# Attention's output from packed rows, its biases folded into one row, and the first transfers issued inside the first normalization

## What is computed

```
x = x + xattn(layernorm(x), ctx)          # W_Q b_Q W_K b_K W_V b_V W_O b_O
   Q = (x W_Q + b_Q), K = (ctx W_K + b_K), V = (ctx W_V + b_V), by head
   out = concat_h( softmax(Q K^T / 4) V ) W_O + b_O
x = x + ssm(layernorm(x), ...)
x = x + experts(layernorm(x), ...)
```

## Time and profile before

| | |
|---|---|
| median of 3 runs | 2363.89 us |
| the profiled execution's own time | 2363.51 us |
| its span, first to last instruction | 2361.8 us |
| TensorE busy | 2154.9 us (91%) |
| VectorE / ScalarE / GpSimd busy | 61% / 52% / 34% |
| mean granted TensorE clock | 0.956 of full |

### The profile page before, as it was taken

The page is one execution under the profiler, slowest core; times in us unless marked ns, Lnnn a source line. Parts: engine busy times, 40 slices in busy tenths (PEclk is TensorE's granted clock), DMA queues, the critical chain, the costliest instruction groups (busy, mean ns, idle before and its releaser), DMA issues. The chain is left out here.

```text
span 2361.8 us, 65032 instructions
## 1 busy us (share of the span) xinstructions
PE 2154.9 (91%) x28672; PEld 1768.7 (75%) x28672; DVE 1444.9 (61%) x2610; ACT 1239.7 (52%) x1667; POOL 797.4 (34%) x571
## 2 busy tenths in 40 slices
PE   5999999999999999999999997896799997499993
PEld 3789999999999999999999995643233336499993
DVE  4655556555555555565555552427588875688885
ACT  2355555555555555555555553363799971255661
POOL 2222222222222222222222212012699962255551
PEclk8999999999999999999999998987899998699997
DMA  2111111111111111111111103004875521466663
GB/s 90 36 49 46 40 48 39 47 42 39 47 42 40 51 42 41 48 39 47 41 39 48 43 16 103 4 5 185 216 173 145 143 81 55 158 223 224 223 221 123
DMA packets 130685, 197.40 MB, mean 84 GB/s; under 512 B 17714, under 2 KB 108850, under 8 KB 130243
## 3 DMA queue, kind: packets, MB, share of 16 engines
q1 hardware_dynamic: 120594, 176.58, 24.9%
q0 software_dynamic: 4416, 12.06, 1.5%
q10 hardware_dynamic: 5392, 4.59, 0.6%
HBM read 161.60 MB, written 31.59 MB: 82 GB/s over the span
## 5 line engine op out<-in xcount | busy, mean ns | idle before, releaser
L507 DVE TENSOR_REDUCE max_part<-work 128x1 f32<-128x384 f32 (+1 forms) x1024 | 539.2, 570 | 239.7 <-PE work L635 216.2
L570 ACT ACTIVATE probs<-scores 128x1024 f32<-128x1024 f32 (+1 forms) x416 | 423.8, 1026 | 397.5 <-PE scores L660 381.5
L467 POOL TENSOR_TENSOR ctx_lo<-ctx_whole,ctx_hi 128x768 fp32r<-128x768 f32 (+1 forms) x128 | 232.3, 1815 | 1034.2 <-DVE ctx_hi L490 1034.2
L502 DVE SCALAR_TENSOR_TENSOR keys_lo<-work,bk,keys_hi 128x384 fp32r<-128x384 f32 (+1 forms) x256 | 162.6, 636 | 262.2 <-ACT keys_hi L549 262.2
L1193 POOL TENSOR_TENSOR decay<-steps_in,xn 128x1024 f32<-128x1024 f32 x126 | 243.2, 1965 | 53.4 <-DMA steps_in<-scratch_results 39.7
L625 PE MATMUL work<-wv_hi,ctx_hi 128*128 128x256 f32 (+1 forms) x832 | 243.9, 293 | 2.1
L654 PE MATMUL scores<-q_hi,keys_hi 64*128 64x256 f32 (+1 forms) x1664 | 241.9, 283 | 0.0
L654 PE MATMUL scores<-q_lo,keys_hi 64*128 64x256 f32 (+1 forms) x1664 | 237.2, 277 | 0.0
L654 PE MATMUL scores<-q_hi,keys_lo 64*128 64x256 f32 (+1 forms) x1664 | 237.1, 277 | 0.0
L625 PE MATMUL work<-wv_hi,ctx_lo 128*128 128x256 f32 (+1 forms) x832 | 234.4, 282 | 0.0
L674 PE MATMUL acc<-probs,values 128*17 128x64 f32 x13312 | 230.5, 220 | 4.0 <-ACT probs L570 4.0
(11 more groups left out here) (234 smaller groups left out, 4685.4 us busy)
## 6 DMA issues: line engine op xcount, KB each, us to landing
xs<-in_w_T SPq DMA_DIRECT2D x46, 1024.0 KB
ctx_whole<-in_ctx_T SPq DMA_DIRECT2D x96, 384.0 KB, 3.2
steps_in<-scratch_results SPq DMA_DIRECT2D x256, 128.0 KB, 2.7
ctx_whole<-in_ctx_T SPq DMA_DIRECT2D x32, 449.0 KB, 3.5
scratch_results<-steps SPq DMA_DIRECT2D x16, 512.0 KB, 2.6
scratch_mixed<-mixed ACTq DMA_DIRECT2D x32, 128.0 KB, 1.7
mixed_b<-scratch_mixed SPq DMA_DIRECT2D x4, 1024.0 KB, 13.6
scratch_z<-z SPq DMA_DIRECT2D x16, 256.0 KB, 2.5
```

What stands on the lines that cost most here:

```text
L467: nc.gpsimd.tensor_tensor(ctx_lo[c][:, :, 0:n], s.ctx_whole[c % 2][:, :, 0:n], ctx_hi[c][:, :, 0:n].bitcast(F32), ALU.subtract).then_inc(l ...
L502: nc.vector.scalar_tensor_tensor(keys_lo[par][:, m, start:start + n], bank[:, 0:n], s.bk[:, m:m + 1], keys_hi[par][:, m, start:start + n]. ...
L507: nc.vector.reduce_max(max_part[par][:, place(pair), c:c + 1], bank[:, 0:CHUNKS[c][1]], AX) \
L570: nc.scalar.activation(probs[slot][0:rows, :], scores[slot][0:rows, :], ACT.Exp, scale=1.0 / HD ** 0.5).then_inc(exp_done, 1)
```

## The change

1. `load_constants` is gone. Its transfers become `sp_start` of the first normalization and its identity part of `pool_start`. W_O, b_V and b_O are loaded there as well, ahead of the context.
2. b_V W_O is made once at the end of that block: VectorE widens b_V to 128 equal columns, TensorE multiplies it by W_O (two matmuls of 256 columns), VectorE adds it to `bo`, which holds b_O in every partition.
3. In attention, GpSimd adds `bo` to four tiles of `x_tok` at the end of each of the passes b = 2 to 5.
4. The head groups' places in the columns of the result are permuted (`mixed_column`), and `attention_output` loads only filled rows, packed: 8 transfers of 16 partitions x 8 batches x 128 columns for each group (32 in place of 4). `mixed_b`, `mixed_T` and `wo` are half as large. `row_of` is made by VectorE from `ident` in four pieces. A token tile is spread by 4 matmuls of 128 columns, the two halves into output partitions 0 to 63 and 64 to 127, and projected by 2 matmuls, each tile as soon as it is divided.
5. ScalarE's bias and loads, GpSimd's clearing, selector and addition leave the block.

```diff
-TOKENS_LOADED, MIXED_LOADED, RESULTS_LOADED = 16, 32, 48
+TOKENS_LOADED, MIXED_LOADED, RESULTS_LOADED = 16, 16 * 9, 16 * 10
...
+            sp.dma_start(s.wo[:, :, :], d.W_O.rearrange("(a p) n -> p a n", p=P)).then_inc(s.o_loaded, 16)
+            sp.dma_start(s.bv[:, :], column_tiles(d.b_V), allow_slow_non_contiguous=True).then_inc(s.o_loaded, 16)
+            sp.dma_start(s.bo[:, :], d.b_O.rearrange("(a n) -> a n", a=1).to_broadcast([P, DIM])).then_inc(s.o_loaded, 16)
+            sp.wait_ge(context_padded, 1)
             for c in range(2):
                 load_context(sp, d, s, 0, c)
...
+            dve.wait_ge(s.o_loaded, 48)
+            nc.vector.tensor_copy(bv_wide[:, :, :], s.bv[:, :].rearrange("p (g a) -> p g a", a=1)
+                                  .to_broadcast([P, KD, P])).then_inc(bv_widened, 1)
+            dve.wait_ge(bias_projected, 1)
+            nc.vector.tensor_tensor(s.bo[:, :], s.bo[:, :], banks[0][:, 0:DIM], ALU.add)
+
+        def project_bias(pe):
+            pe.wait_ge(s.o_loaded, 48)
+            pe.wait_ge(bv_widened, 1)
+            pe.wait_ge(copied, KD * LN_GROUPS - 3)
+            for g in range(KD):
+                last = nc.tensor.matmul(banks[0][:, 0:DIM], bv_wide[:, g, :], s.wo[:, g, :],
+                                        start=(g == 0), stop=(g == KD - 1))
+            last.then_inc(bias_projected, 1)
...
+            def add_bias(first, last):
+                for t in range(first, last):
+                    nc.gpsimd.tensor_tensor(s.x_tok[:, t, :], s.x_tok[:, t, :], s.bo[:, :], ALU.add)
+
             prepare(0, 0)
             for b in range(1, batches):
                 prepare(b, b % 2, more=b + 1 < batches)
+                if 2 <= b < 2 + LN_GROUPS:
+                    add_bias((b - 2) * GT, (b - 1) * GT)
...
-                sp.dma_start(mixed[:, batches, :, :].rearrange("p b g l -> p b (g l)"),
-                             d.mixed.rearrange("b p n -> p b n")[:, batches, :]).then_inc(s.group_loaded[c], 16)
+                for half in range(2):
+                    for j in range(HPG):
+                        first = half * SIDE + j * HD
+                        sp.dma_start(mixed[first:first + HD, batches, :],
+                                     d.mixed.rearrange("b p n -> p b n")[32 * j:32 * j + HD, batches,
+                                                                         half * P:(half + 1) * P]) \
+                            .then_inc(s.group_loaded[c], 16)
...
-        def add_values_bias(act, c):
-            act.wait_ge(divided, CT * (c + 1))
-            for g in range(G):
-                part = mixed_T[:, g, c * BANK:(c + 1) * BANK]
-                nc.scalar.activation(part, part, ACT.Identity, bias=bv[:, g:g + 1]).then_inc(biased, 1)
...
-            nc.gpsimd.memset(row_of[:, :, :], 0.0).then_inc(row_of_made, 1)
-            pool.wait_ge(row_of_made, 1)
-            nc.gpsimd.affine_select(out=row_of[:, :, :], in_=row_of[:, :, :], compare_op=ALU.not_equal, fill=1.0,
-                                    base=0, pattern=[[-1, P], [0, 32]], channel_multiplier=1) \
-                .then_inc(row_of_made, 1)
-            pool.wait_ge(loaded, 16 * 9)
-            nc.gpsimd.tensor_tensor(s.x_tok[:, :, :], s.x_tok[:, :, :],
-                                    bo[:, :].rearrange("p (a n) -> p a n", a=1).to_broadcast([P, TT, DIM]), ALU.add) \
-                .then_inc(bias_added, 1)
...
-                    last = nc.tensor.matmul(spread[t % SPREAD_RING][:, i, :],
-                                            row_of[:, 4 * b:4 * b + 4, :].rearrange("p j i -> p (j i)"), inverse[:, :],
-                                            start=True, stop=True)
+                    for half in range(2):
+                        last = nc.tensor.matmul(spread[t % SPREAD_RING][half * SIDE:(half + 1) * SIDE, i, :],
+                                                row_of[:, 4 * b:4 * b + 4, :].rearrange("p j i -> p (j i)"),
+                                                inverse[:, half * P:(half + 1) * P],
+                                                start=True, stop=True, skip_group_check=True)
...
-            pe.wait_ge(biased, G * (c + 1))
             for t in range(CT * c, CT * (c + 1)):
+                pe.wait_ge(divided, t + 1)
...
+        def make_rows(c):
+            rows = slice(c * 4 * CB, (c + 1) * 4 * CB)
+            nc.vector.tensor_copy(row_of[:, rows, :], s.ident[:, rows].rearrange("p (q a) -> p q a", a=1)
+                                  .to_broadcast([P, 4 * CB, HD])).then_inc(row_of_made, 1)
```

More of the change, by code:

```diff
@@ L234, in _ @@
             for c in range(2):
                 load_context(sp, d, s, 0, c)
-        @block.gpsimd
-        def _(pool):
-            nc.gpsimd.memset(s.ident[:, :], 0.0).then_inc(filled, 1)
-            pool.wait_ge(filled, 1)
-            nc.gpsimd.affine_select(out=s.ident[:, :], in_=s.ident[:, :], compare_op=ALU.not_equal, fill=1.0,
-                                    base=0, pattern=[[-1, P]], channel_multiplier=1).then_inc(filled, 1)
-def load_context(sp, d, s, b, c):
-    start, size = CHUNKS[c]
-    sp.dma_start(s.ctx_whole[c % 2][:, :, 0:size],
-                 d.ctx_T[bass.ds(b, 1), :, start:start + size]
-                 .rearrange("a (k p) s -> p (a k) s", p=P)).then_inc(s.ctx_loaded[c % 2], 16)
@@ L252, in normalize_and_project_queries, with pe_before @@
[L252 to L263 removed]
+        def pe_before(pe, g):
+            if g == 0:
+                pe.wait_ge(ident_made, 2)
@@ L764, in act_start @@
-        def act_start(act):
-            act.dma_start(bo[:, :], d.b_O.rearrange("(a n) -> a n", a=1).to_broadcast([P, DIM])).then_inc(loaded, 16)
-            act.wait_ge(cleared, 2)
-            for j in range(4):
-                rows = slice(32 * j, 32 * j + HD)
-                act.dma_start(wo[rows, :, :], d.W_O.rearrange("(g c e) n -> c e g n", c=4, e=HD)[j]) \
-                    .then_inc(loaded, 16)
-                act.dma_start(bv[rows, :], d.b_V.rearrange("(g c e) -> c e g", c=4, e=HD)[j],
-                              allow_slow_non_contiguous=True).then_inc(loaded, 16)
-            act.wait_ge(loaded, 16 * 9)
-            add_values_bias(act, 0)
```

105 lines of the change are left out of this document (56 added, 49 removed).

## The result

The changed kernel takes 2348.08 us, the median of 4 runs (2344.87 to 2351.42); the kernel before takes 2363.55 us beside it. The ratio is 0.9935, with a 95% interval of 0.9918 to 0.9952, so it is 11 to 19 us faster. The profiled execution took 2349.55 us with a span of 2347.8, 14.0 less than before; the forecast of -17.9 was made for this difference.

| part of the span | forecast | measured | from, before and after |
|---|---|---|---|
| start, to attention's first instruction | -4.2 | -4.7 | 36.90 and 32.19 |
| attention's first batch, to its first store | 0 | +2.9 | 94.60 and 97.45 long |
| additions in four passes | +5.3 | +6.7 | 43.2 and 44.86 a pass |
| the rest, to the output block | 0 | +0.5 | start 1455.49 and 1460.77 |
| output block, to `s_bank`'s first matmul | -19.0 | -19.6 | 71.81 and 52.24 long |

What follows compares the result with a forecast made beforehand. Attention was taken as bound by TensorE alone, the output block as a chain by turns. Terms -4.2 + 5.3 - 19.0 = -17.9 against 2363.51 gave 2345.6 us, 2346.0 on the median; range 2339 to 2355.

Steps and rivals of the forecast that it cites:

- Start, -4.2: Kernel start: statistics 5.0 us sooner, bias row at the block's end costs 0.8; -4.2 us, bounds -3.0 and -4.6.
- Additions, +5.3: Attention: GpSimd's additions ahead of the masked queries make TensorE wait 1.3 us in four passes; +5.3 us, bounds +4.8 and +8.8.
- I take 0.575: Attention: one GpSimd addition of 128x256 taken at 0.575 us, 2.3 us for four.
- Output block, -19.0: Output block: gains sum to -20.5 us, 1.5 given back for the clock; -19.0, bounds -23 and -12.
- The beginning: Output block, group 0: first division at 1463, last addition at 1473.6 in place of 1483.11; -9.5 us.
- The two cycles: Output block, groups 1 and 2: 9.5 us from one group's last addition to the next, against 15.6 and 13.9 before.
- 1.5 had been given back: Output block: 1.5 us allowed for the clock behind the second cycle's 3.0 us pause and the first's longer one.
- Group 3: Output block, last group: three tiles wait ready, the fourth needs the first's addition; 6.0 us against 7.8, -1.8.
- Narrow loads: Rival, output block: 16-partition transfers pass one at a time; slower kernel from 1.66 us each (4%), 0.8 to 1.66 (10%).
- Queue: Output block: 32 loads put the SSM weights 6 us behind their place, about 1487 in place of 1481; hidden.
- four signs of being wrong: VectorE waiting for `mixed_b` after group 0, clock 0.5 in projections, GpSimd's addition far from 0.58 us, SyncE's weights ending last.
- not low throughout, which had 6%: Rival, output block: the clock case, a granted clock of 0.5 in the projections; chance 6%.

Runs made afterwards that it cites:

- two queues: Against the kernel with the additions behind the masks: the 32 packed loads split, lower halves issued by SyncE, upper by ScalarE; 2340.53 us, ratio 0.9902.
- the filled first batch: Against the kernel with the additions behind the masks: idle matmuls before attention's first unit (7) and first row maximum (15); 2343.86 us, ratio 0.9922.
- the additions behind the masks: Against the changed kernel: GpSimd's four additions moved from ahead of the next batch's masked queries to right behind them, passes 3 to 6; 2338.36 us, ratio 0.9888.

## Why the prediction was nearly right

It gave 2346.0, between 2339 and 2355; the median is 2348.08. By its own steps:

- **Start, -4.2.** Measured -4.7 in the profiled execution. The first quarter's landing released VectorE at 4.77, as costed, and the bias row at the block's end cost 0.6 instead of the 0.8 taken, in every kernel that has it. In the ten kernels with the changed start, attention begins at 32.2 to 33.5 us, 32.9 in the mean; in the two with the old one at 36.9 and 37.4. The means differ by the forecast 4.2. That it comes out to the tenth is luck: the first query projection took 4.1 to 5.3 us in the ten, at a granted clock that reads 1.00 for the shortest and the longest, so why it differs is not shown; and the -4.7 is the best of them, just past the bound of -4.6.
- **Additions, +5.3.** The mechanism was right, four passes and no other, and the loss came back whole when only the place was changed. The size was off: +6.65, within the bounds (4.8 to 8.8). The term took a 128x256 addition at 0.575 us, near a sixteenth of the large one. It is 0.70 from start to start, 0.744 by itself, nearer to the upper row, two of 128x128. So the step "I take 0.575" is what failed. The first masking operation now starts 4.88 us behind the start of the last chunk's subtraction (172.39 to 177.27), before 2.23 (174.26 to 176.49): 2.65 us more in each pass where 2.3 had been taken, 4 x 0.35 = 1.4, and that reached TensorE.
- **Output block, -19.0.** Measured -19.6. The beginning gave more: -11.5 against the -9.5 for group 0. The first division came 6.4 us after the block's start rather than 7.5, and group 0's projection started 11.9 us after it rather than 14.0. The two cycles gave less, -3.6 and -2.8 against -4.8 and -4.4, a shortfall of 2.8 for which 1.5 had been given back, besides the 1.3 already in the first cycle. That 1.3 makes the -4.8 of the sum out of the -6.1 that 9.5 against 15.6 gives. It was the author's estimate for the clock behind the pause of 3.31 us, 0.50 at 1489 to 1491, and no run shows it: in the changed kernel the spreading and projection behind that pause took 0.88 and 1.63 more. Behind the second pause, reckoned at 3.0 us and 2.87 in the trace, they took 0.88 and 0.75 more: the granted clock was 0.50 and 0.51 in the spreadings behind both pauses, not only behind the longer. Group 3 gave -1.8, as forecast. The two errors cancel, so the sum was better than its parts. The tile's spreading was 0.51 us where 0.5 had been taken, so 1.7 times faster than 0.86, as taken. The reason given, that the two halves overlap, is not shown to be the whole of it: a repeated matmul of 128 columns took 0.177 us and not the 0.22 reckoned from the projection's by columns, and from there to 0.128 it is 1.4 times.
- **Narrow loads.** The rival needed 0.8 us a load to count as one; it is 0.50. Still, the loads held VectorE 1.48 and 1.16 us in the first two groups, and with two queues the first projection came 1.1 us sooner. On one queue the issue sets the pace, 0.50 us a load, since two queues issue at 0.47 each at the same time. With two queues the median time to landing grew from 2.5 us to 4.5 and 4.7, so there something behind the issue begins to count; no run isolates what.
- **Queue.** The first weight's issue came at 1477.27, 16.5 us after the block's start, and before 8.7 (1455.88 + 8.32 - 1455.49): 7.8 later, where 6 had been forecast. But the weights' issues behind it went faster, that of `win` in 0.43 us instead of 4.84, and the last was issued 23.4 us after the block's start, before 24.9 (1480.40). That 2 MB stand ahead of them instead of 4 may be the reason; it was not tested. Hidden either way.
- **Its own signs.** Of the four signs of being wrong three came: VectorE waited for `mixed_b` after group 0 (1.16 us), the clock was at 0.50 for part of two projections (0.69 and 0.83 in their mean, 1.00 in group 0's, so not low throughout, which had 6%), and GpSimd's addition took 0.70 and not 0.58. `ssm_projections` started 14.3 us sooner (1513.01), not 16 to 19. So the number is better than the account, since the block's beginning, 2 us better than forecast, made up for much of it.
- **Not foreseen.** +2.9 us in attention's first batch, most likely by the granted clock (0.68 and 0.83 in two windows, before 0.99 and 0.97). That no term had it is fair for the middle of the range; it belongs into its width.

Of the -14.0 in the profiled spans, -17.9 had been forecast; 2.9 of the 3.9 between them are the first batch, 1.35 the additions' size, 0.8 two seams, and the start and the block give 1.1 back.

## What to carry to other kernels

Work that is put on an idle engine must be placed behind that engine's last hand-over to the bottleneck, not ahead of it: the same sixteen additions cost 6.65 us in one place and nothing a few lines further on, or at the start of a later block. A long wait in the profile is worth only the distance to the next late thing: 12.4 us of waiting, 4.8 us of possible start, 2.5 us gained alone, and much more once the next two waits had gone as well. With idle matmuls in two short pauses the granted clock was 1.00 in the pauses and behind them, in both kernels that had them, without a gain in time that is clear of noise by themselves; where they started 4 us into a pause and ran at 0.82, they ran past the work that they were to bridge and cost time.

## What the runs showed of the hardware that was not expected

The granted clock behind one and the same pause differed from one kernel's execution to the next. Four of the kernels have the changed output block untouched, with pauses of 3.74 and 2.87 us. Behind the second pause the projection took 4.47 us in the changed kernel (granted clock 0.83), 5.65 in the one with the start undone (0.64), 4.57 in the one with the filled first batch (0.80), and 3.72 in the one with the additions behind the masks (1.00). Their blocks took 52.2, 52.2, 51.2 and 49.1 us; of that the spreading and projection behind the two pauses are 13.8, 13.9, 13.0 and 11.1, so most of the difference is in them. One pause's length does not decide the clock behind it: 2.87 us was followed by 0.51, 0.50, 0.54 and 1.00 in the spreading.

A matmul of 128 columns into 64 output partitions took 0.177 us where each was issued three times in a row, and 0.128 in turn with one into the other 64, both at a granted clock of 1.00. Against 0.22 by columns, the two places give 1.7 times and the mixing's four places of 32 give 2.7. How much of either is overlap the runs don't separate.
